# A recommender kernel on one core: preparation in another order, the last group taken row by row, fillers and averages on TensorE

## The reference

```python
items_emb = item_table[items]; user_emb = user_table[users]; hist_emb = user_table[history_users]
scores = einsum('bhd,bd->bh', hist_emb, user_emb)
user_his_emb = einsum('bh,bhd->bd', scores, hist_emb)
x = concatenate([items_emb, user_his_emb, user_emb], axis=1)        # 2048 x 384
x = _dice(_batchnorm(x @ W1 + b1, g1, be1), a1)                     # 2048 x 1024
x = _dice(_batchnorm(x @ W2 + b2, g2, be2), a2)                     # 2048 x 512
y = x @ W3 + b3                                                     # 2048 x 1
def _dice(x, alpha):
    avg = x.mean(axis=1); var = sum((x - avg) ** 2 + 0.001, axis=1)
    ps = sigmoid((x - avg) / sqrt(var))
    return ps * x + (1.0 - ps) * alpha * x
```

## Time and profile before

| | us |
|---|---|
| median of 3 runs | 794.44 (794.24 to 794.94) |
| the profiled execution | 794.12 |
| its span | 792.3 |

### The profile page before, as it was taken

One profiled execution on the slowest core, in us unless ns is written; L12 is line 12 of the kernel. 1 busy time (PEld: TensorE's weight loads), 2 busy tenths in 40 slices (PEclk: granted clock), 3 DMA queues, 4 the chain that ended last, 5 costly groups with the idle time before them and its releaser, 6 DMA issues.

```text
span 792.3 us, 17056 instructions
## 1 busy us (share of the span) xinstructions
PE 585.3 (74%) x3685; PEld 548.1 (69%) x3685; DVE 520.2 (66%) x1345; ACT 357.9 (45%) x880; POOL 481.9 (61%) x507
## 2 busy tenths in 40 slices
PE   2765678586859576686868878876746899999793
PEld 1664677476858576686868868766635788888683
DVE  8763658384756748476575775774466979974473
ACT  3033345353535344343434544534547857743552
POOL 6377777777777777777777777777711243421025
PEclk9886598787778797877879869788775989999997
DMA  7222222222212122212122222221200000000000
GB/s 228 62 53 51 53 55 55 54 53 51 55 53 55 52 53 54 52 53 54 51 54 55 54 52 53 55 54 52 53 11 0 1 1 1 1 0 1 1 1 0
DMA packets 17606, 34.62 MB, mean 44 GB/s; under 512 B 8472, under 2 KB 8768, under 8 KB 17536
## 3 DMA queue, kind: packets, MB, share of 16 engines
q0 software_dynamic: 14720, 29.14, 14.5%
q1 hardware_dynamic: 2816, 4.66, 1.7%
HBM read 33.76 MB, written 0.01 MB: 43 GB/s over the span
## 4 chain that ended last, share of the span: by engine, by line
issue 29%; PE 28%; DMA 15%; POOL 12%; DVE 9%; ACT 3%; POOLq 1%; DVEq 1%; ACTq 0%; SPq 0%; PEldq 0%
DMA rows<-in_L_rec_user_table_dram,slot_idx 14%; PE ps L1279 13%; POOL rows L465 12%; PE ps L1232 3%; PE ps L1156 2%; PE ps L1339 2%; PE ps L1172 2%; PE ps L1219 2%; DVE prod L736 1%; ACT wide L1123 1%; DVE work L742 1%; PE ps L1334 1%; ACT scaled L1039 1%; DVE stats L729 1%; PE ps L1147 1%
## 5 line engine op out<-in xcount | busy, mean ns | idle before, releaser
L465 POOL DMA_INDIRECT rows<-in_L_rec_user_table_dram,slot_idx x432 | 410.5, 950 | 133.0 <-issue 113.3
L1232 PE MATMUL ps<-ident,scaled 128*128 128x128 f32 x984 | 180.3, 334 | 130.5 <-ACT scaled L1039 130.5
L1039 ACT ACTIVATE scaled<-rows,work 128x128 f32 (+1 forms) x492 | 175.2, 400 | 198.2 <-DVE work L746 149.9
L1232 PEld LDWEIGHTS ps<-ident,scaled 128*128 128x128 f32 x984 | 156.6, 232 | 146.0 <-issue 137.3
L736 DVE TENSOR_TENSOR prod<-rows,ps 128x512 f32<-128x512 f32 x123 | 84.3, 685 | 133.5 <-POOLq L472 116.2
L1279 PE MATMUL ps<-h,w 128*128 128x256 f32 (+1 forms) x576 | 119.4, 369 | 1.2 <-DVE h L867 1.2
L1279 PEld LDWEIGHTS ps<-h,w 128*128 128x128 f32 x576 | 103.2, 200 | 13.1 <-DVE h L867 1.5
L742 DVE TENSOR_REDUCE work<-prod 128x512 f32 (+1 forms) x123 | 84.3, 686 | 22.1 <-DVE prod L736 17.5
L1156 PE MATMUL ps<-wide,h 128*128 128x103 f32 x512 | 77.7, 318 | 0.0
L1156 PEld LDWEIGHTS ps<-wide,h 128*128 128x128 f32 x512 | 76.0, 236 | 0.1
L508 POOL TENSOR_SCALAR work<-work,rest,alphas 128x2048 f32<-128x2048 f32 x7 | 20.1, 2876 | 91.8 <-ACT work L1103 91.8
(11 more groups left out here) (193 smaller groups left out, 757.9 us busy)
## 6 DMA issues: line engine op xcount, KB each, us to landing
rows<-in_L_rec_user_table_dram,slot_idx POOLq DMA_INDIRECT x432, 2.5
w<-in_L_rec_W_dram SPq DMA_DIRECT2D x1, 2048.0 KB, 14.9
w<-in_L_rec_W_dram SPq DMA_DIRECT2D x1, 1536.0 KB, 7.9
h<-in_r_history_users_dram SPq DMA_DIRECT2D x2, 400.0 KB, 3.4
out_dram<-y_col,perm POOLq DMA_INDIRECT x16, 2.1
wide<-in_L_rec_user_table_dram,own_idx POOLq DMA_INDIRECT x5, 5.8
wide<-in_L_rec_item_table_dram,own_idx POOLq DMA_INDIRECT x5, 5.2
last_row<-in_L_rec_user_table_dram SPq DMA_DIRECT2D x1, 64.0 KB, 3.5
```

Source lines behind the costliest of these rows:

```text
L465: nc.gpsimd.indirect_dma_start(rows[:, s, :], None, user_table, bass.IndirectOffsetOnAxis(slot_idx[:, s:s + 1], 0)).then_inc(landed[s], 16)
L1039: nc.scalar.activation(scaled[:, j, :], rows[:, bass.ds((g & (GROUPS - 1)) * GROUP + j, 1), :], ACT.Copy, scale=score[:, bass.ds(g * GROUP ...
L1232: nc.tensor.matmul(pooled_ps, scaled[:, j, :], ident[:, :], start=False, stop=False, skip_group_check=True).then_inc(slot_summed, 1)
```

## The change

- GpSimd: the iota `slot_no` moves ahead of the own rows' gathers. `arrived` counts rows and not groups. The mix of the gate goes.
- ScalarE: both `own_moved` permissions are given at the start; a dry Sign activation stands ahead of the index work; `ranked` is copied ahead of `perm`; `w3_diag` is made in tile 0 and not before it.
- VectorE: the first two rounds of the sort come ahead of the own rows' places; the matrices of tile 1 ahead of the plan; parameters are taken after the second group of tile 0. In the last tile the statistics of the earlier tiles are taken after four groups, and the last group is weighed row by row (`weigh_end`).
- The gate is `(ps + alpha / (1 - alpha)) * x` in one operation, and the factor `1 - alpha` goes into ScalarE's copies of layer 2.
- TensorE: of the fillers ten now stand ahead of the ranking and five behind; `keep_busy` adds 8 before the last group, 12 after the last layer 1, 5 and 10 beside chunk 0's variance. Chunks 2 and 3 get their averages by eight products (DIRECT = 4) and no column sums.

```diff
-FILLERS = 12
+FILLERS = (10, 5)
...
+    DIRECT = 4
...
+    nc.gpsimd.iota(slot_no, [[1, COLS]], base=0, channel_multiplier=0,
+                   allow_small_or_imprecise_dtypes=True).then_inc(slot_no_made, 1)
...
             gather_own(i, own_rows[i][:, s, :], own_idx[:, s + i * TILES:s + i * TILES + 1])
-            if i == 0 and s == 0:
-                nc.gpsimd.iota(slot_no, [[1, COLS]], base=0, channel_multiplier=0,
-                               allow_small_or_imprecise_dtypes=True).then_inc(slot_no_made, 1)
     pool.wait_ge(most_ready, 1)
...
             pool.wait_ge(landed[q * GROUP + j], count)
-            pool.sem_inc(arrived if j == GROUP - 1 else passed, 1)
+            pool.sem_inc(arrived, 1)
...
     def step(i, live):
-        if live(2) and i - 2 >= NARROW:
-            c = i - 2
-            pool.wait_ge(gated, c + 1)
-            nc.gpsimd.tensor_scalar(dev_of(c), dev_of(c), rest[:, 0:1], alphas[:, 0:1],
-                                    ALU.mult, ALU.add).then_inc(mixed, 1)
...
         dve.wait_ge(own_ranked, i + 1)
-    own_more = [more_of(dve, i) for i in range(2)]
-    find_own_places(0, 0)
...
         cut_top(0, r)
+    own_more = [more_of(dve, i) for i in range(2)]
+    find_own_places(0, 0)
+    dve.wait_ge(rows_placed, 1)
+    find_places(1, 0)
+    find_places(1, 1)
+    find_own_places(1, 0)
...
-    dve.wait_ge(rows_placed, 1)
-    find_places(1, 0)
-    find_places(1, 1)
-    find_own_places(1, 0)
...
+    def take_parameters():
...
     def weigh(g, t, op, bound, feed=False, round_no=None):
-        hold(dve, arrived, g + 1)
+        hold(dve, arrived, g * GROUP + GROUP)
...
+    def weigh_end(g, t, bound):
+        for j in range(GROUP):
+            hold(dve, arrived, g * GROUP + (j + 1))
+            one = bass.ds(g * GROUP + (t * GROUP + j), 1)
+            nc.vector.tensor_tensor(prod[:, j:j + 1, :], rows[:, bass.ds((g & (GROUPS - 1)) * GROUP + j, 1), :],
+                                    user_now.unsqueeze(1), ALU.mult).then_inc(end_multiplied, 1)
+            dve.wait_ge(end_multiplied, j + 1)
+            nc.vector.tensor_reduce(raw[:, one], prod[:, j:j + 1, :], AX_X, ALU.add).then_inc(end_dotted, 1)
+            dve.wait_ge(end_dotted, j + 1)
+            nc.vector.scalar_tensor_tensor(score[:, one], slot_no[:, bass.ds(g * GROUP + j, 1)], bound, raw[:, one],
+                                           ALU.is_lt, ALU.mult).then_inc(end_scored, 1)
...
-            with dve.Fori(0, g1 - g0) as r:
+            with dve.Fori(0, GROUPS) as r:
+                weigh(group(r), t, ALU.is_ge, from_begin, True)
+            layer1_stats(t - 1)
+            dve.wait_ge(stats_done, M1 * t)
+            for m in range(M1):
+                nc.vector.bn_aggr(mv[:, m, :], stats1[:, m, 0:t, :].rearrange("p t s -> p (t s)")).then_inc(bn_step[0], 1)
+            with dve.Fori(GROUPS, g1 - g0) as r:
                 weigh(group(r), t, ALU.is_ge, from_begin, True)
         else:
...
                 find_own_places(i, t + 1)
+            if t == 0:
+                take_parameters()
...
-        if t:
+        if t and t + 1 < TILES:
             layer1_stats(t - 1)
-        weigh(g1, t, ALU.is_lt, ends_f[:, t + 1:t + 2])
-    dve.wait_ge(stats_done, M1 * (TILES - 1))
-    for m in range(M1):
-        nc.vector.bn_aggr(mv[:, m, :], stats1[:, m, 0:TILES - 1, :].rearrange("p t s -> p (t s)")).then_inc(bn_step[0], 1)
+        if t < TILES - 1:
+            weigh(g1, t, ALU.is_lt, ends_f[:, t + 1:t + 2])
+        else:
+            weigh_end(g1, t, ends_f[:, t + 1:t + 2])
...
-            if c < NARROW:
-                dve.wait_ge(gated, c + 1)
-                nc.vector.tensor_scalar(dev_of(c), dev_of(c), rest[:, 0:1], alphas[:, 0:1],
-                                        ALU.mult, ALU.add).then_inc(mixed_first, 1)
-                dve.wait_ge(mixed_first, c + 1)
-            else:
-                dve.wait_ge(mixed, c - NARROW + 1)
-            nc.vector.tensor_tensor(h1[:, :, chunk(c)], by_block(dev_of(c), M1), h1[:, :, chunk(c)],
-                                    ALU.mult).then_inc(dice_done, 1)
+            dve.wait_ge(gated, c + 1)
+            if c == 0:
+                dve.wait_ge(par_ready, 6)
+            nc.vector.scalar_tensor_tensor(h1[:, :, chunk(c)], by_block(dev_of(c), M1), over[:, 0:1], h1[:, :, chunk(c)],
+                                           ALU.add, ALU.mult).then_inc(dice_done, 1)
...
-        if live(0) and i >= NARROW:
+        if live(0) and i >= DIRECT:
             half = by_block(col_tree[:, 0:4 * spans[i][1]], 4)
...
 def _(act):
+    for moved in own_moved:
+        act.sem_inc(moved, 1)
     act.wait_ge(consts_made, N_CONSTS)
+    nc.scalar.activation(root_dry[:, :], ones[:, 0:1], ACT.Sign).then_inc(dried, 1)
     halves = [slice(i * (n_idx // 2), (i + 1) * (n_idx // 2)) for i in range(2)]
...
-        nc.scalar.activation(perm[:, t:t + 1], rows_ps[:, PERSON:PERSON + 1], ACT.Copy).then_inc(perm_kept, 1)
...
         nc.scalar.activation(ranked[:, t % 2, :], rows_ps, ACT.Copy).then_inc(tile_kept, 1)
+        nc.scalar.activation(perm[:, t:t + 1], rows_ps[:, PERSON:PERSON + 1], ACT.Copy).then_inc(perm_kept, 1)
...
     for i in range(2):
-        act.sem_inc(own_moved[i], 1)
         with act.Fori(0, more_of(act, i)) as s:
             hold(act, own_landed[i], s * 16 + (OWN_SLOTS + 1) * 16)
             nc.scalar.activation(own_rows[i][:, bass.ds(s + OWN_SLOTS, 1), :], next_row[:, i, :], ACT.Copy).then_inc(own_moved[i], 1)
...
-    act.wait_ge(par_ready, 2)
-    act.wait_ge(slot_no_made, 3)
-    for k in range(M2):
-        nc.scalar.activation(w3_diag[:, k, :], ident[:, :], ACT.Copy, scale=w3c[:, k:k + 1]).then_inc(w3_spread, 1)
...
     def scale_rows(g, t, after):
-        hold(act, scored, g + (t + 1))
+        by_slot = t == TILES - 1 and after is end_scaled
+        if not by_slot:
+            hold(act, scored, g + (t + 1))
         for j in range(GROUP):
+            if by_slot:
+                act.wait_ge(end_scored, j + 1)
...
+        if t == 0:
+            act.wait_ge(par_ready, 2)
+            for k in range(M2):
+                nc.scalar.activation(w3_diag[:, k, :], ident[:, :], ACT.Copy, scale=w3c[:, k:k + 1]).then_inc(w3_spread, 1)
...
                 nc.scalar.activation(h2[:, k, chunk(c)], l2_ps[c % 2][:, k, 0:w], ACT.Identity,
-                                     bias=b2c[:, k:k + 1]).then_inc(l2_kept, 1)
+                                     bias=b2c[:, k:k + 1], scale=rest[:, 0:1]).then_inc(l2_kept, 1)
...
+    def warm_up(count):
+        for _ in range(count):
+            nc.tensor.matmul(filler_ps, ident[:, :], not_before[:, :], start=True, stop=True)
+    pe.wait_ge(hist_fixed, 2)
+    warm_up(FILLERS[0])
     pe.wait_ge(bins_counted, 1)
     nc.tensor.matmul(bins_ps, ones[:, :], bin_rows[:, :], start=True, stop=True).then_inc(bins_summed, 1)
     nc.tensor.matmul(before_ps, not_before[:, :], bin_rows[:, :], start=True, stop=True).then_inc(bins_summed, 1)
-    for _ in range(FILLERS):
-        nc.tensor.matmul(filler_ps, ident[:, :], not_before[:, :], start=True, stop=True)
+    warm_up(FILLERS[1])
...
+    def keep_busy(count):
+        for _ in range(count):
+            nc.tensor.matmul(idle_ps, ident[:, :], ident[:, :], start=True, stop=True)
...
+        if t == TILES - 1:
+            keep_busy(8)
...
     layer1_pooled(TILES - 1)
+    keep_busy(12)
     pe.wait_ge(w2_loaded, 16)
...
-            if c < NARROW:
+            if c < DIRECT:
                 for k in (*range(M1 - len(by_other(c))), *by_other(c)):
                     if k in by_other(c):
-                        pe.wait_ge(normed_other if c else normed_first, k - by_other(c).start + 1)
+                        pe.wait_ge(normed_other if c else normed_first, (others(c - 1) if c else 0) + k - by_other(c).start + 1)
                     else:
                         pe.wait_ge(normed_act, sum(M1 - len(by_other(x)) for x in range(c)) + k + 1)
                     mm = nc.tensor.matmul(avg_ps[c % 2][:, 0:w], mean_of1[:, :], h1[:, k, chunk(c)],
                                           start=(k == 0), stop=(k == M1 - 1))
                 mm.then_inc(avg_ready, 1)
             else:
-                pe.wait_ge(col_summed, c - NARROW + 1)
+                pe.wait_ge(col_summed, c - DIRECT + 1)
...
             mm.then_inc(var_ready, 1)
+            if c == 0:
+                keep_busy(5)
...
             mm.then_inc(inv_spread, 1)
+            if c == 0:
+                keep_busy(10)
```

52 lines of the change are left out of this document (28 added, 24 removed).

## The result

| | before | changed |
|---|---|---|
| median | 794.4 (4 runs) | 785.62 (784.56 to 786.5, 4 runs) |
| ratio, 95% interval | | 0.9888 [0.9873, 0.9904] |
| the profiled execution | 794.12 | 784.56 |
| its span | 792.3 | 782.8 |

What follows compares the result with a forecast made beforehand. The prediction took an unbroken GpSimd queue of 432 indirect DMAs, untouched by the change, as the bound; 8.6 + 1.6 + 1.2 + 1.6 + 2.9 - 0.1 = 15.8 us off 794.12 gave 778.3, median 778.6, range 775.3 to 784.9.

Steps and rivals of the forecast that it cites:

- Part 1: Before the gather stream: first row gather near 25.1 in place of 33.88; gain 8.6 us, bounds 5.8 and 9.0.
- keys at full clock: Start: TensorE places the sorted keys from 19.6 to about 23.6, keys near 24.7, before GpSimd asks at 25.1.
- the prediction's own sign of being wrong: Start of the stream: the prediction would be wrong if the first gather waits for idx_ready past 26.
- The rival's 5.9 for cold keys: Start: with keys placed at TensorE's lower clock or the ring halted, part 1 gives 5.9; total 781.3, chance 0.14.
- I take back 1.0: Start: of 1.5 us VectorE lost at a cast beside the iota, 1.0 comes back once the iota moves.
- a ring with 0.8 us to spare: Stream's 17th gather: its buffer is free at 44.3, wanted at 45.1, so the ring does not stop.
- Part 2: Last group, weighed slot by slot with VectorE's statistics moved up: gain 1.6 us, bounds 1.0 and 2.2.
- Part 3: Fillers hold TensorE's clock: 1.2 us in the last layer 1, 1.6 in chunk 0's averages; bounds 0 and 1.8 each.
- part 4: Layer 2: fewer column sums, no gate mix, more TensorE products; gain 2.9 us, bounds -1.2 and 4.3.
- The 2.11 us sum: Layer 2: VectorE's sum of squares for chunk 2, stalled beside GpSimd's mix (0.42 for a later chunk), loses that stall.
- the clock is not held: Rival: fillers fail; parts 3 nearly nothing, part 4 nothing, part 2 only 1.3; 784.2 us, chance 0.19.
- The stream gains less: Rival: cold placing of keys, or the ring halted at its 17th gather; part 1 gives 5.9, 781.3 us, chance 0.14.

Runs made afterwards that it cites:

- fourteen fillers: The changed kernel with fourteen TensorE fillers behind the ranking in place of five; 782.03 us, ratio 0.9839.
- iota late: The changed kernel with the slot numbers' iota moved behind the own rows' gathers; 784.04 us, ratio 0.9877.
- own places first: The changed kernel with the register loads and tile 0's own places ahead of the first sort again; 783.64 us, ratio 0.9857.
- statistics back: The changed kernel with the eight aggregations of earlier tiles' statistics behind the last group again, still weighed row by row; 781.73 us, ratio 0.983.
- two-chunk run: The changed kernel with DIRECT = 2, averages of chunks 2 and 3 by VectorE's column sums again; 782.09 us, ratio 0.9846.

## Why the prediction was wrong

- **Part 1, keys at full clock: the step that failed most.** This made 2.6 us of part 1's miss of 3.8, and the prediction's own sign of being wrong came: the first gather waited past 26. I had the placing begin at 19.6 and end at 23.6. It began at 20.84 and ended at 26.26. The clock is 1.63 us of the 2.66 (fourteen fillers). The rest is the late start, 1.24, which was the late indices for the most part in this profile and the iota in the others (iota late: 1.30). With both mended it is at 19.54 and 23.33, so the walk was sound and its two assumptions false. I never reckoned where the five fillers end, and argued from the number of products ahead of the placing ("fifteen") and not from the idle time behind them. The rival's 5.9 for cold keys is near the 6.22 gained at the first gather; the stream took 1.39 of it back, and the part measured 4.83, below the forecast's bound of 5.8.
- **Part 1, "I take back 1.0" of VectorE's loss.** Nothing came back: the iota moved the loss from the cast to the mending. The first own gather came at 7.63, and at 6.33 with the iota late.
- **Part 1, a ring with 0.8 us to spare.** It stopped, for 1.07 us more than the usual 0.30, and the stream took 1.39 us longer (543.67 from the first gather to the last, 542.28 before). From the first sort to the first weighing VectorE took 18.5 us (26.65 to 45.13), where my sum had 17.4 (the sort 2.6 earlier, the weighing 2.0) and before 16.8. The loads and own places cost what I took (2.7; 2.5 by own places first, where the stretch took 15.95 and the ring didn't stop). The 1.1 us that the sum lacks stand behind the plan: with tile 1's matrices moved ahead of it, VectorE is idle for 0.94 us at 37.91, between writing `tile_slots` (L694) and the loop whose length it reads from there. Before, the matrices filled that place. This reading is from the timelines (own places first has the same 0.94); no run tests it. Nor do the runs show the stop in the total: the stream took 542.3 to 544.7 us in the five profiles without a stop, and 543.4 to 544.9 in the nine with one.
- **Part 2.** Row by row was sized within its bounds (1.6; 2.2 measured with the statistics back, the upper bound). What failed is "VectorE's eight statistics, which stood here, are moved up": I named the work and gave it no price at its new place, where 5.1 us of VectorE stand ahead of the last two groups. It took 2.5 back.
- **Part 3 (2.8) and part 4 (2.9)** measured 2.43 and 2.79. By the profiles their cause is the clock, as forecast: without fillers layer 1 and the averages are near the values before. But inside part 3 two errors cancel: layer 1 gave 1.7 (1.2 forecast) and the averages, with a fall of the clock in them, 0.9 (1.6). Part 4 has the right size in part by luck: 1.9 us of it hang on where the clock falls, and by the two-chunk run the averages on TensorE, which I had reckoned in its favour, cost a little. The 2.11 us sum is gone (0.42 in the changed kernel).
- Chunk 0's three additions took 1.00, 0.66 and 0.53 us for 0.69, 0.42 and 0.29, beside GpSimd's sixteen normalising operations: 0.8 us longer, where I took nothing. By the Trainium skill ("SBUF — State Buffer", SBUF: two separate sides) each could have waited for a whole one, 1.7 in all; the trace has about half of that, as waits for the rest of one already begun would give; no row tells which.
- The rival "the clock is not held" had the nearest total (784.2) for the wrong reason: its losses are in parts 3 and 4, which came out near the forecast. "The stream gains less" named both places; it took 2.7 us off part 1 where 3.8 were lost, because it took the two as alternatives, and they came together.
